# A graph-attention kernel: attention scores in f32 between the last input products, input products in column groups, edge loads first on their queue

## The reference, cut to what matters

```python
x1 = relu(x @ W_ah + b_ah)
def gat_conv(x, src, dst, W, a_src, a_dst, b):
    h = (x @ W).reshape(N, H, C)
    as_n = (h * a_src).sum(-1)                 # scores of sources
    ad_n = (h * a_dst).sum(-1)                 # scores of targets
    e = leaky_relu(as_n[src] + ad_n[dst], 0.2)
    m = segment_max(e, dst)
    p = exp(e - m[dst])
    s = segment_sum(p, dst)
    alpha = p / (s[dst] + 1e-16)
    return segment_sum(alpha[:, :, None] * h[src], dst).reshape(N, H * C) + b
xs = [relu(gat_conv(x1, ..., W_l, ...)) for l in 0..2]
out = layernorm(x + relu(concat(xs) @ W_out + b_out))
```

## Time and profile before

| | |
|---|---|
| median of 3 runs | 1050.19 us |
| profiled execution | 1052.09 us, span 1050.4 us |
| PE busy | 971.5 us, 92% |
| DVE busy | 760.8 us, 72% |
| ACT busy | 373.6 us, 36% |
| mean granted TensorE clock | 0.98 |
| chain that ended last | begins at 812.7 us, nearly all TensorE |

### The profile page before, as it was taken

One profiled execution on the slowest core, in us unless ns is written; L12 is line 12 of the kernel. 1 busy time (PEld: TensorE's weight loads), 2 busy tenths in 40 slices (PEclk: granted clock), 3 DMA queues, 4 the chain that ended last, 5 costly groups with the idle time before them and its releaser, 6 DMA issues. The chain is left out here.

```text
span 1050.4 us, 14553 instructions
## 1 busy us (share of the span) xinstructions
PE 971.5 (92%) x5638; PEld 910.9 (87%) x5638; DVE 760.8 (72%) x1059; ACT 373.6 (36%) x541; POOL 22.0 (2%) x34
## 2 busy tenths in 40 slices
PE   0699999799999968899999999999999999999997
PEld 0577765789999968899999999999999968999996
DVE  4699974835999992999899899898887554423322
ACT  0445432212122211555554646555555381101100
POOL 1000000000000000000100100001001010000000
PEclk9999999889999988899999999999999999999999
DMA  9600041424443426222531714423934154332200
GB/s 226 144 6 4 1 166 47 149 67 129 149 128 117 138 94 181 64 86 86 119 90 37 150 57 110 85 86 75 354 88 111 38 117 162 103 118 79 98 30 30
DMA packets 65346, 108.10 MB, mean 103 GB/s; under 512 B 17219, under 2 KB 49060, under 8 KB 64271
## 3 DMA queue, kind: packets, MB, share of 16 engines
q1 hardware_dynamic: 43700, 66.36, 20.9%
q0 software_dynamic: 4048, 18.60, 7.5%
q10 hardware_dynamic: 17547, 22.44, 7.5%
HBM read 80.31 MB, written 27.08 MB: 102 GB/s over the span
## 5 line engine op out<-in xcount | busy, mean ns | idle before, releaser
L1216 PE MATMUL ps<-R_W 125*125 125x193 f32 x2400 | 399.6, 328 | 9.2 <-DVE R_W L919 5.8
L1216 PEld LDWEIGHTS ps<-R_W 125*125 125x125 f32 x2400 | 393.1, 188 | 12.8 <-ACT R_XIN L643 6.6
L627 ACT ACTIVATE R_W<-R_EXP,s 125x1250 f32<-125x1250 f32 x120 | 161.2, 1344 | 164.8 <-PE ps L1216 97.0
L919 DVE SCALAR_TENSOR_TENSOR R_W<-R_W,R_CNT 125x1250 f32<-125x1250 f32 x120 | 174.4, 1453 | 4.3 <-DVE R_EXP L908 2.4
L878 DVE CUSTOM_DVE_ANT_0 R_ROWS<-R_MASK,R_ROWS 125x1250 bf16<-125x1250 bf16 x100 | 138.5, 1454 | 3.2 <-ACTq L580 3.2
L1174 PE MATMUL ps<-Wl_hi,x_hi 128*125 128x384 f32 x360 | 124.6, 346 | 5.6 <-DVE Wl_lo L839 5.6
L1174 PE MATMUL ps<-Wl_lo,x_hi 128*125 128x384 f32 x360 | 123.9, 344 | 0.0
L1174 PE MATMUL ps<-Wl_hi,x_lo 128*125 128x384 f32 x360 | 123.8, 344 | 0.0
L1287 PE MATMUL ps<-Wo_hi,xs_hi 128*125 128x384 f32 x324 | 109.5, 338 | 0.3 <-PE ps L1265 0.3
L1287 PE MATMUL ps<-Wo_lo,xs_hi 128*125 128x384 f32 x324 | 109.2, 337 | 0.0
L1287 PE MATMUL ps<-Wo_hi,xs_lo 128*125 128x384 f32 x324 | 109.2, 337 | 0.0
(11 more groups left out here) (152 smaller groups left out, 833.8 us busy)
## 6 DMA issues: line engine op xcount, KB each, us to landing
xs_dram<-R_XIN POOLq DMA_DIRECT2D x18, 625.0 KB, 10.2
h_dram<-R_HOUT ACTq DMA_DIRECT2D x30, 336.0 KB
R_W<-h_dram SPq DMA_DIRECT2D x12, 840.0 KB
R_ROWS<-as_dram SPq DMA_DIRECT2D x12, 625.0 KB, 3.7
R_EXP<-u_dram SPq DMA_DIRECT2D x6, 1250.0 KB, 6.3
R_X<-u_dram SPq DMA_DIRECT2D x6, 1250.0 KB, 6.0
R_ROWS<-in_W_all SPq DMA_DIRECT2D x18, 384.0 KB, 4.8
Wo_sb<-in_W_out POOLq DMA_DIRECT2D x1, 6912.0 KB, 28.1
```

The costliest lines, as they stand in the source:

```text
L627: nc.scalar.activation(prob[r % PSLOTS], expo[:, r % XSLOTS], ACT.Exp, bias=s02[:, r % NT, ds(2 * p + r // NT, 1)]).then_inc(S["exp_done"], 1)
L919: nc.vector.scalar_tensor_tensor(out=prob[r % PSLOTS], in0=prob[r % PSLOTS], scalar=HUGE, in1=cntT[:, r % NT], op0=ALU.min, op1=ALU.mult). ...
L1216: ins = mm(ps[0:PT, o:o + HW], prob[r % PSLOTS][:, t * PT:(t + 1) * PT], hB[:, q, j], start=(j == 0 and t % 2 == 0), stop=(j == NT - 1), s ...
```

## The change

- SP: the load of aB and of slices 0 to 2 of layer 0 moves from ahead of the edge loads to behind their second batch; slices 3 to 5 are loaded behind all edge loads. The raw weights of h part 0 are loaded behind slice 0 of layer 2 (was: slice 1 of layer 1), those of part 1 behind the last slice, when x1 is done.
- ScalarE issues its loads in the order x group 0, W_ah tiles 0 and 1, x group 1, W_ah 2 and 3, x group 2, W_ah 4 and 5, with a semaphore for each W_ah tile.
- x1 has column groups of 500, 500 and 250 nodes. The six products of group 0 come first, then groups 1 and 2 for each m. The transposes of x group 0 and the whole first product stand ahead of window 0; groups 1 and 2 are transposed after products 1 and 2, in the same turns of banks 5 to 7. A step stands behind each window from window 0 on.
- V: all 144 reductions stand behind the windows on VectorE.
- Scores: 18 f32 matmuls (24 output rows) from V and x1T, feature tiles 0 to 2 behind product 15 (with a wait for the whole of V), 3 to 5 behind product 17. The split copies V_hi and V_lo with their padding are gone. x1_lo of a tile waits for its scores, since it overwrites x1T.
- scores_turn and more_counts come after tile 0 of part 0; more_counts stands ahead of `rest_w(1)` on VectorE, and its buffers lie elsewhere. `Wl_hi0` lies where the one-hots were, and is rounded after product 15.
- U_AT is 6; the first exp stands ahead of the last h copy on ScalarE.

```diff
-XT_AT = (2, 4, 6)
-X1_FROM = 8
+X1_HEAD = 6
-X1_STEPS = KT * len(COLS) * KT
+X1_ORDER = [(m, 0) for m in range(KT)] + [(m, g) for m in range(KT) for g in (1, 2)]
+X1_STEPS = KT * len(X1_ORDER)
+XT_AFTER = (-1, 1, 2)
...
 PARTS = 2 * LAYERS
-ASAD_AT = 3
...
-U_AT = 3
+U_AT = 6
...
-    return min(max(w + 1 - X1_FROM, 0), X1_STEPS)
+    return min(X1_HEAD + w + 1, X1_STEPS)
+
+
+def xT_use(g):
+    return KT * g + max(XT_AFTER[g] + 1, 0)
+
+
+def x1_use(i):
+    return i + KT * sum(i > a for a in XT_AFTER)
+
+
+def x1_whole(m):
+    return x1_use(KT + 2 * m + 1) + 1
 
...
-            sp.dma_start(aB.rearrange("p w f -> p (w f)"),
-                         a_all[0:1].rearrange("l w f -> l (w f)").broadcast_to((KP, 2 * D))).then_inc(a_in[0], 16)
-            for k in range(VSLOTS):
-                sp.dma_start(Wv[:, k], W_all[0, k * KP:(k + 1) * KP]).then_inc(wv_in[k], 16)
...
-
+                if i == 1:
+                    sp.dma_start(aB.rearrange("p w f -> p (w f)"),
+                                 a_all[0:1].rearrange("l w f -> l (w f)").broadcast_to((KP, 2 * D))).then_inc(a_in[0], 16)
+                    for k in range(VSLOTS):
+                        sp.dma_start(Wv[:, k], W_all[0, k * KP:(k + 1) * KP]).then_inc(wv_in[k], 16)
+
+            for k in range(VSLOTS, KT):
+                load_v(0, k)
             for l in range(1, LAYERS):
                 sp.wait_ge(S["v_made"], 2 * HEADS * KT * l)
                 sp.dma_start(aB.rearrange("p w f -> p (w f)"),
                              a_all[l:l + 1].rearrange("l w f -> l (w f)").broadcast_to((KP, 2 * D))).then_inc(a_in[l], 16)
                 for k in range(KT):
                     load_v(l, k)
-                    if (l, k) == (1, 1):
-                        sp.wait_ge(S["x1_ps"], KT * len(COLS) // 2)
+                    if (l, k) == (2, 0):
+                        sp.wait_ge(S["turn_ps"], x1_whole(2))
                         sp.dma_start(w_raw[0], w_half(0)).then_inc(S["w_in"], 16)
-                    if (l, k) == (2, 0):
-                        sp.wait_ge(S["x1_ps"], KT * len(COLS))
-                        sp.dma_start(w_raw[1], w_half(1)).then_inc(S["w_in"], 16)
-
+
+            sp.wait_ge(S["turn_ps"], x1_whole(KT - 1))
+            sp.dma_start(w_raw[1], w_half(1)).then_inc(S["w_in"], 16)
             more, each = passes(sp)
             with sp.Fori(0, more) as t:
                 with sp.Fori(0, each) as w:
...
+            load_x(0)
+            load_w_ah(0)
+            load_w_ah(1)
+            load_x(1)
+            load_w_ah(2)
+            load_w_ah(3)
+            load_x(2)
+            load_w_ah(4)
+            load_w_ah(5)
...
 
+            def xT_out(g):
+
+                t0, w = GROUPS[g]
+                for k in range(KT):
+                    use = xT_use(g) + k
+                    act.wait_ge(S["turn_ps"], use + 1)
+                    nc.scalar.copy(xT[:, k, t0 * PT:(t0 + w) * PT], bank(5 + use % 3)[:, 0:w * PT]).then_inc(S["turn_sb"], 1)
...
-                                     ).then_inc(S["x1_sb"], 1)
-                nc.scalar.activation(x1_hi[:, m, o:o + w], bank(5 + i % 3)[:, 0:w], ACT.Relu, bias=b_ah_sb[:, m:m + 1]
-                                     ).then_inc(S["x1_sb"], 1)
-
+                m, g = X1_ORDER[i]
+                o, w = GROUPS[g][0] * PT, GROUPS[g][1] * PT
+                use = x1_use(i)
+                act.wait_ge(S["turn_ps"], use + 1)
+                nc.scalar.activation(x1T[:, m, o:o + w], bank(5 + use % 3)[:, 0:w], ACT.Relu, bias=b_ah_sb[:, m:m + 1])
+                nc.scalar.activation(x1_hi[:, m, o:o + w], bank(5 + use % 3)[:, 0:w], ACT.Relu, bias=b_ah_sb[:, m:m + 1]
+                                     ).then_inc(S["turn_sb"], 1)
+                if i in XT_AFTER:
+                    xT_out(XT_AFTER.index(i))
+
+            xT_out(0)
             act.wait_ge(S["small_in"], 32)
+            for i in range(X1_HEAD // KT):
+                x1_out(i)
...
                 act.wait_ge(S["w_in"], 16 * n + 16)
                 nc.scalar.copy(Wl_hi[n][:], w_raw[n]).then_inc(S["w_hi"], 1)
 
-            round_w(0)
+            for i in range(x1_upto(NW - 1) // KT + 1, len(X1_ORDER)):
+                x1_out(i)
+                if i == W0_AT:
+                    act.wait_ge(S["win_done"], NW)
+                    round_w(0)
+            act.wait_ge(S["v_made"], 2 * HEADS * KT * LAYERS)
+            act.wait_ge(S["asad_ps"], KT)
+            for g, (t0, w) in enumerate(GROUPS):
...
                         round_w(n + 1)
-                    if n == 0 and t == ASAD_AT:
-                        scores_out()
-                    if n == 0 and t == ASAD_AT + 1:
+                    if n == 0 and t == 0:
                         more_masks()
+                    if n == PARTS - 1 and t == NT - 2:
+                        exp_tile(0, 0)
...
-            for k in range(VSLOTS):
-                reduce_v(0, k)
...
 
-            for k in range(VSLOTS, KT):
-                reduce_v(0, k)
-            for k in range(KT):
-                reduce_v(1, k)
+            for l in range(LAYERS):
+                for k in range(KT):
+                    reduce_v(l, k)
+            rest_w(0)
             for m in range(KT):
-                dve.wait_ge(S["x1_sb"], 2 * len(COLS) * (m + 1))
+                dve.wait_ge(S["turn_sb"], x1_whole(m))
+                dve.wait_ge(S["asad_ps"], m + 1)
                 nc.vector.tensor_tensor(x1_lo[:, m], x1T[:, m], x1_hi[:, m].bitcast(f32), ALU.subtract
                                         ).then_inc(S["x1_lo"], 1)
-            rest_w(0)
-            link(nc.vector.memset(zeros, 0.0))
-            for pad in (V_hi, V_lo):
-                nc.vector.tensor_copy(pad[:, :, 2 * LH:KP], zeros.unsqueeze(1).broadcast_to((KP, KT, KP - 2 * LH))
-                                      ).then_inc(S["v_pad"], 1)
-            for k in range(KT):
-                reduce_v(2, k)
-            dve.wait_ge(S["v_hi"], 1)
-            nc.vector.tensor_tensor(V_lo[:, :, 0:2 * LH], V, V_hi[:, :, 0:2 * LH].bitcast(f32), ALU.subtract
-                                    ).then_inc(S["v_lo"], 1)
+            more_counts()
             rest_w(1)
-            more_counts()
 
...
-                    pe.wait_ge(S["xT_sb"], KT * len(GROUPS))
-                if k == 0 and i >= 3:
-                    pe.wait_ge(S["x1_sb"], 2 * (i - 2))
-                ins = mm(bank(5 + i % 3)[:, 0:w], W_ah_sb[m][:, k], xT[:, k, o:o + w], start=(k == 0), stop=(k == KT - 1))
+                m, g = X1_ORDER[i]
+                o, w = GROUPS[g][0] * PT, GROUPS[g][1] * PT
+                if k == 0:
+                    take_turn(x1_use(i))
+                    pe.wait_ge(wah_in[m], 16)
+                    pe.wait_ge(S["turn_sb"], xT_use(g) + KT)
-
+                    ins.then_inc(S["turn_ps"], 1)
+                    if i in XT_AFTER:
+                        xT_group(XT_AFTER.index(i))
+
+            xT_group(0)
+            for s in range(X1_HEAD):
+                x1_step(s)
...
 
+            def scores(k):
+
+                pe.wait_ge(S["turn_sb"], x1_whole(k))
+                for g, (t0, w) in enumerate(GROUPS):
+                    ins = mm(ps[0:2 * LH, (2 + g) * BANK:(2 + g) * BANK + w * PT], V[:, k], x1T[:, k, t0 * PT:(t0 + w) * PT],
+                             start=(k == 0), stop=(k == KT - 1))
+                ins.then_inc(S["asad_ps"], 1)
+
...
+                    pe.wait_ge(S["mask_ready"], 2 * NT)
+                    pe.wait_ge(S["v_made"], 2 * HEADS * KT * LAYERS)
+                    for k in range(KT // 2):
+                        scores(k)
+            for k in range(KT // 2, KT):
+                scores(k)
...
                     ins.then_inc(S["h_ps"], 1)
-                    if n == 0 and t == ASAD_AT:
-                        scores()
-                    if n == 0 and t == ASAD_AT + 1:
+                    if n == 0 and t == 0:
```

More of the change, by code:

```diff
@@ L46 @@
 PARTS = 2 * LAYERS
-ASAD_AT = 3
+SCORES_AT = 15
+W0_AT = 15
 ROUND_AT = 4
@@ L262, in gnn_program @@
         x_in = [sem(f"x_in{g}") for g in range(len(GROUPS))]
+        wah_in = [sem(f"wah_in{m}") for m in range(KT)]
         win_in = [sem(f"win_in{i}") for i in range(len(BATCHES))]
@@ L492, in _, with load_x @@
         def _(act):
-            for g, (t0, w) in enumerate(GROUPS):
+            def load_x(g):
+                t0, w = GROUPS[g]
                 for rows in ROWS16:
@@ L496, in _, with load_w_ah @@
                                   ).then_inc(x_in[g], 16)
-            for m in range(KT):
+            def load_w_ah(m):
                 act.dma_start(W_ah_sb[m], W_ah.rearrange("(k p) f -> p k f", p=KP)[:, :, m * KP:(m + 1) * KP]
-                              ).then_inc(S["wah_in"], 16)
+                              ).then_inc(wah_in[m], 16)
+            load_x(0)
[7 more added lines that the diff above has]
+            load_w_ah(5)
             def counts_out(i):
@@ L549, in _ @@
```

(25 more changed lines are left out.)

68 lines of the change are left out of this document (23 added, 45 removed).

## The result

The changed kernel takes 1052.92 us (median of 7 runs, 1052.38 to 1054.93), the kernel before 1050.02 us on the same chip (7 runs, 1048.48 to 1050.4): a ratio of 1.0029 with a 95% interval of 1.0018 to 1.0039. The forecast was 1042.0 us with a range of 1036.0 to 1052.5 us, so the time lies just above the range. The profiled execution of the changed kernel has 1052.47 us around a span of 1050.8 us, at a mean granted clock of 0.977. That of before was itself 2 us above its median, so the two spans differ by 0.4 us where the medians differ by 2.9; positions in the two traces are compared with this in mind.

What follows compares the result with a forecast made beforehand. TensorE was taken to bound the kernel, busy 414 of 418.5 us from 425 us on. Start, windows, V, scores, h tiles and shifts summed to a first attention tile 8.2 us earlier; off the 1050.19 us median: 1042.0 us, range 1036 to 1052.5.

Steps and rivals of the forecast that it cites:

- The position of the first attention tile: Start of attention on TensorE: its move counts fully at the end; from 425.24 to 417.0 us, 8.2 us earlier.
- V's reductions: VectorE after the windows: 144 reductions, 40.3 us, with idle and load waits 53.9 us, from 136.0 to 189.9 us.
- Rival A: Kernel start: ScalarE free only at 34.0 us, its own queue the limit; 1050.8 us, or 1053.2 us; chance 0.20.
- C: Kernel start: ScalarE free at 21.6 us, product 0 in 6.2 us; 5.2 us less, 1036.8 us; chance 0.08.
- B: V's loads: slices land later and the three-slot ring turns slower, 6 us over four refills; 1048.0 us; chance 0.14.
- ScalarE's last issue: Load issue at the start: 1.97 MB less ahead on SP saves 8.8 us, ending at 25.2 us instead of 34.0.
- Product 0: First x1 product on TensorE, ahead of window 0: 7.8 us, partly at half clock; bounds 6.2 and 10.2 us.
- the length of the maxima: VectorE's maxima beside the h tiles: start near 225 us, last 165.9 us as before, done at 391 us.
- the wait at the shifts: TensorE's 13.2 us wait for the attention shifts: gone, since TensorE reaches their new place only at 400.9 us.
- The path to the first exponent: From the shift transposes to the first exponent: 11.3 us before, 10.3 us at full clock, ending at 411.2 us.
- The 8.2 us: Forecast gain of the whole change at the first attention tile: 417.0 us against 425.24 us.
- Rival D: Scores between the last products: V does not stall, 26 + 2.7 us fall away; 1013 us; chance 0.02.

Runs made afterwards that it cites:

- a_v0first: Changed kernel with the attention vectors and three W slices of layer 0 loaded first and reduced ahead of the windows, as before; 1052.77 us, ratio 1.0017.
- b_u6: Kernel before with U_AT = 6 alone; 1041.09 us, ratio 0.9905.
- The square of U_AT: Both kernels at U_AT 3 and 6: U_AT 6 worth 0.95% in the kernel before, 0.88% in the changed; rest of the change costs 1.17% and 1.24%.
- a_noV: Changed kernel with V of one layer only (layers 1 and 2 not loaded or reduced, their scores zeros); 1024.66 us, ratio 0.9758.
- a_u3: Changed kernel with U_AT back at 3; 1063.08 us, ratio 1.0117.
- b_free: Kernel before with Wl_lo at b = 9, ROUND_AT 3, U_AT 5 and h's first loads ahead on SP; 1039.85 us, ratio 0.9902.

## Why the prediction was wrong

*Right, with its mechanism.* The position of the first attention tile is the result. V's reductions take 53.9 us (forecast 53.9) with two idle stretches of 5.78 and 5.74 us (5.4), the scores start at 191.7 us (189.9), TensorE waits 26.2 us for them (26), and the h tiles start at 213.7 us (213.0). Rival A (the head gains nothing) and C (more) are out, and so is B: the V chain was not longer, it began 1.8 us late behind the windows.

*Right with some luck.* ScalarE's last issue ends at 25.2 us, as forecast, but the forecast put all 8.8 us down to SP's bytes, and a_v0first shows at most 6.7 us for them. Product 0 takes 6.95 us (7.8). Up to the h tiles the sum is off by 0.7 us because the later start of V (1.8 us) and the cheaper stretch from the scores to the h tiles (21.9 us, forecast 23.1) nearly cancel. In the other traces with the same head and V chain the last issue ends between 25.3 and 27.6 us, product 0 takes up to 8.17 us and the h tiles start between 214.9 and 217.9 us, so an error under 1 us says little.

*The step that failed: the length of the maxima, and with it the wait at the shifts, put at nothing.* "The maxima start about 3 us later ... near 225, and last 165.9 us: done at 391." The start was right (226.7). The length was read from the first and the last row of the kernel before, as if the stretch between were work. It was 148.2 us of work and 17.5 us of waits for ScalarE's Wl_hi, which go with the h parts, and the h parts were what the change makes later. In the changed kernel the waits are 30.1 us and the maxima end at 405.2 us, 14 us behind the forecast. All rows for it were in the trace of before: the gaps in front of L839, 13.01 and three of 1.5 us. The prediction costed TensorE's waits and left VectorE's own out of the sum: the wait that the lock causes had no term.

*What it became at the end.* The shifts: forecast without a wait at 400.9 us, measured at 407.21; 2.7 us of it because TensorE got there later, 3.65 us as a wait. The path to the first exponent took 11.9 us instead of 10.3. Of these 1.6 us, 1.0 is the clock: I had assumed the full one, and behind the wait it is 0.50, the 1.2 GHz level, so that the ten transposes take 2.26 us instead of the 1.24 us that they take at full clock in b_u6. The other 0.5 us is in the load of u, which takes 7.1 us from its issue to the first exponent (411.97 to 419.08) and took 6.6 us in the kernel before (401.70 to 408.28). The clock:

```profile
407.00:411.00 4.00, 3.79 (x16) 0.50 0.30 106
```

From exponent to attention tile 7.25 us instead of 5.75, because the tile waited for the load of h, which stands on SP behind the load of u and moved with it. 2.7 + 3.65 + 1.6 + 1.5 = 9.4 us, against the measured 426.33 - 417.0 = 9.3 us. The other 1.6 us of the miss of 10.9 us (1052.92 - 1042.0) lie in the base: I took the move off the median of before, but its profiled execution was 1.9 us slower than that median, and the changed kernel's was 0.45 us faster than its own; 0.7 us go the other way, behind the first attention tile (624.5 against 625.2 us).

*What the forecast gain was made of.* The 8.2 us were put down to the whole change. The square of U_AT shows that a gain of this size comes from the new place of the shifts (9 to 10 us by the times of either kernel), and that the rest costs some 12 us. Had I costed this one constant on the kernel before by itself, the sum would have been 13.2 - 3.65 = 9.55 us, measured 10.0, and the question would have been why the rest should cost only 1 us when the h parts come later (TensorE reaches tile 6 of the last part at 393.0 us in b_u6, and my own sum had it at 400.9 us in the changed kernel).

*Rival D* (V doesn't stall) stood at 1013 us, 29 us under the forecast. a_noV confirms the size, 28.3 us against the 26 + 2.7 = 28.7 us given. The slower rival, A, had the right sign for a wrong reason: the head did what it should. No rival named the lock.

*Left open.* Whether V can be made whole by 165 us without giving back the start: a_noV leaves its work out, and a_v0first only moved it. That would need the reductions of layers 1 and 2 at another place or on another engine, and it wasn't tried. Also open is why the executions of one and the same head differ by some 4 us at the start of the h parts.

## What to carry to other kernels

A stretch on one engine between its first and its last row is a length only when the waits inside it are taken out and given to whoever causes them; list the waits of the engine whose stretch you move, not only of the one that bounds the kernel. When a wait comes out the same to the hundredth in two versions (3.65 and 13.20 us here), ask whether two engines are locked to each other; if they are, as here, only the start of the one that leads, or the place of the lock, is worth anything. When two traces are compared by position, first take off what they already differ by ahead of the edit: in a_u3 that was 3.0 us of 7.7. Cost a changed constant by itself on the old kernel before crediting its gain to the restructuring around it.

## What the runs showed of the hardware

- A small store behind four strided loads (twice 840 and 98 KB in pieces of 768 B) on the same queue took 8.3 us until its completion let the next load go (8.6 us in b_free), against 2.0 us when it stood first.
- What SP loads first shows in the times of ScalarE's queue. With 1.97 MB less ahead, ScalarE's last issue of W_ah ended at 25.2 us (25.2 to 27.6 us in the seven traces with this head); with the loads of V's first slices back ahead and the same list on ScalarE, at 31.9 us (one trace). The kernel before, which issues x and W_ah in another order, had 34.0 us (33.6 to 34.5 us in six traces). Issuing itself was held: one group of two issues took 8.66 us in the changed kernel and 13.54 us in a_v0first.
- The edge loads, 8 KB each, have no load of V ahead of them on SP's queue now. The first was issued at 16.52 us (16.29 us before), and they still reached VectorE only at 30.69 us, against 31.12 us before: their place in their own queue was not what held them. Their median over the whole kernel is 1.8 us.
- The same wait of 3.65 us left TensorE at another clock. In the changed kernel the granted clock was 0.50 from 407 us on, with the transposes behind the wait (407.21 us). In b_u6 the transposes behind the wait (396.63 us) still ran at full speed, and the clock fell behind them: 0.70 from 397 to 399 us, 0.50 from 399 to 401 us, 0.95 from 401 to 403 us.
